# Moving four uses of a shared matmul bank between slots, with other VectorE positions and more filler products, in an attention and expert kernel

## The reference

```python
q, k, v = heads(ln(x) @ Wq + bq), heads(ln(x) @ Wk + bk), heads(ln(x) @ Wv + bv)
y  = softmax(causal(q @ k.T / sqrt(8))) @ v
qc, kc, vc = heads(ln(x) @ Wcq + bcq), heads(ctx @ Wck + bck), heads(ctx @ Wcv + bcv)
y += softmax(qc @ kc.T / sqrt(8)) @ vc
x  = x + y @ Wp + bp
h  = ln(x)
shared = silu(h @ w1.T) * (h @ w2.T) @ w3.T
scores = sigmoid(h @ router.T); top 2 of scores + expert_bias
x  = x + shared + sum over chosen experts of gate * expert(h)
```

## Time and profile before

| | us |
|---|---|
| median of 3 runs | 451.9 (451.32 to 452.56) |
| profiled execution, its time | 452.91 |
| its span, first to last instruction | 451.2 |
| TensorE busy | 401.8 |
| VectorE busy | 351.0 |
| ScalarE busy | 195.8 |
| GpSimd busy | 77.4 |

### The profile page before, as it was taken

One profiled execution on the slowest core, in us unless ns is written; L12 is line 12 of the kernel. 1 busy time (PEld: TensorE's weight loads), 2 busy tenths in 40 slices (PEclk: granted clock), 3 DMA queues, 4 the chain that ended last, 5 costly groups with the idle time before them and its releaser, 6 DMA issues.

```text
span 451.2 us, 10427 instructions
## 1 busy us (share of the span) xinstructions
PE 401.8 (89%) x3759; PEld 298.0 (66%) x3759; DVE 351.0 (78%) x1186; ACT 195.8 (43%) x326; POOL 77.4 (17%) x139
## 2 busy tenths in 40 slices
PE   0579998999899989999899998999889998998986
PEld 0457565667577667767577756767577766765986
DVE  4477676855898877996989787987889788884877
ACT  5135554453433554355443544553444553444221
POOL 4012001400222021210222013110231003201120
PEclk9999899967899998999999989999899999999999
DMA  5631101110201111110201110110101110000000
GB/s 145 198 103 39 54 25 61 58 31 1 84 0 55 48 42 41 41 41 17 81 0 52 47 54 27 52 47 6 64 8 49 42 59 15 1 25 0 2 13 12
DMA packets 28478, 19.63 MB, mean 44 GB/s; under 512 B 6680, under 2 KB 26272, under 8 KB 28448
## 3 DMA queue, kind: packets, MB, share of 16 engines
q1 hardware_dynamic: 27296, 19.02, 13.0%
q10 hardware_dynamic: 1152, 0.20, 0.4%
HBM read 5.58 MB, written 1.05 MB: 15 GB/s over the span
## 4 chain that ended last, share of the span: by engine, by line
PE 51%; DVE 26%; ACT 12%; issue 8%; DMA 1%; SPq 1%; DVEq 0%; POOL 0%; ACTq 0%; POOLq 0%
PE Y L574 10%; ACT probs L793 8%; PE Bk L426 8%; PE Cb L426 6%; DVE masked_s L1030 6%; PE S L450 5%; PE A L426 4%; DVE act L915 4%; DVE shifts L1036 4%; PE Cb L657 3%; PE S L468 3%; ACT th L773 3%; DVE qs L1005 2%; DVE acc L955 2%; PE Y L541 2%
## 5 line engine op out<-in xcount | busy, mean ns | idle before, releaser
L793 ACT ACTIVATE probs<-S 128x1024 f32<-128x1024 f32 (+1 forms) x128 | 112.3, 917 | 54.1 <-PE S L452 53.4
L780 ACT COPY yT<-Y 128x256 f32<-128x256 f32 x64 | 23.9, 373 | 133.8 <-PE Y L574 133.8
L1036 DVE TENSOR_REDUCE shifts<-S 128x4 f32<-128x1024 f32 x64 | 75.2, 1216 | 1.0 <-PE S L468 0.7
L574 PE MATMUL Y<-probs,vs 128*32 128x256 f32 (+1 forms) x1024 | 67.4, 384 | 9.2 <-DVE qs L1005 6.9
L1030 DVE CUSTOM_DVE_ANT_0 masked_s<-S,later_keys 128x256 f32<-128x256 f32 (+1 forms) x256 | 73.4, 352 | 1.4 <-PE S L464 1.3
L915 DVE SCALAR_TENSOR_TENSOR act<-th,A 128x512 f32<-128x512 f32 x42 | 28.7, 683 | 38.2 <-ACT th L773 38.1
L450 PE MATMUL S<-qs,qk 32*128 32x256 f32 x256 | 46.5, 398 | 10.1 <-DVE shifts L1030 7.6
L1080 POOL TENSOR_SCALAR_AFFINE_SELECT probs<-probs 128x1024 f32<-128x1024 f32 x32 | 35.2, 1100 | 108.5 <-ACT probs L793 108.5
L574 PEld LDWEIGHTS Y<-probs,vs 128*32 128x32 f32 x1024 | 27.9, 114 | 34.2 <-DVE qs L1005 17.4
L426 PEld LDWEIGHTS Bk<-w3T,hid 128*128 128x128 f32 x336 | 41.5, 194 | 13.0 <-DVE hid L924 12.2
L426 PE MATMUL Bk<-w3T,hid 128*128 128x128 f32 x336 | 49.2, 290 | 0.6 <-DVE hid L924 0.6
(11 more groups left out here) (148 smaller groups left out, 689.5 us busy)
## 6 DMA issues: line engine op xcount, KB each, us to landing
qk<-nat SPq DMA_DIRECT2D x192, 64.0 KB, 1.9
xin<-in_x_dram SPq DMA_DIRECT2D x8, 128.0 KB, 2.3
w_raw<-in_L_ffn_w_dram SPq DMA_DIRECT2D x4, 256.0 KB
xres<-in_x_dram SPq DMA_DIRECT2D x8, 128.0 KB, 2.3
out_dram<-acc SPq DMA_DIRECT2D x8, 128.0 KB, 1.8
cin<-in_ctx_dram SPq DMA_DIRECT2D x8, 64.0 KB, 2.0
w_raw<-in_L_ffn_shared_w_dram SPq DMA_DIRECT2D x4, 128.0 KB
w_raw<-in_L_ffn_w_dram SPq DMA_DIRECT2D x1, 512.0 KB
```

The costliest lines, as they stand in the source:

```text
L574: mm = nc.tensor.matmul(Y[QUAD * j:QUAD * (j + 1), q0:T], vs[:, kind, kt, GH * g + j, :], probs[u % 2][:, j, kt * T:(kt + 1) * T - q0], st ...
L793: nc.scalar.activation(probs[s % 2][:, hs, 0:kept(s)], S[:, hs, 0:kept(s)], ACT.Exp, scale=SCALE).then_inc(exped[s], 1)
L1036: nc.vector.tensor_reduce(dst.rearrange("p q j -> p j q"), S[:, hs, :].rearrange("p j (q k) -> p j q k", q=NT), AX_X, ALU.max).then_inc(re ...
```

## The change

Of the uses of bank Cb, cT goes from late in slot 4 to early in slot 4, v from early in slot 5 to late in slot 4, and qkc from early in slot 6 to early in slot 7. TensorE makes the early use in slots without a pair too, ahead of the transposed maxima. On VectorE the activation stands behind qs in all slots with a pair; the statistics of the first layer norm go from slot 7 to the start of slot 6, `compare` stands behind them ahead of qs, `choose` goes to the end of slot 7, and the addition of qkc stands between the two halves of slot 7's maxima. GpSimd's `rstd` for the first layer norm and both steps of `route` are in slot 6. The fillers get a count for each half: in slot 7 one in the second half of the scores and one in each half of the maxima; in turn 0, and in turn 1 up to slot 4, slot 4 has two where it had one.

```diff
@@ -54,8 +54,8 @@
-EARLY = [("xT", 1), ("tokens3", -1), ("yT", -1), ("vc", 0), None, ("v", 1), ("qkc", 1), None]
-LATE = [("tokens2", -1), ("qk", 1), ("out", -1), ("x2T", -1), ("cT", 1), ("route", -1), ("tokens0", 0), ("tokens1", 0)]
+EARLY = [("xT", 1), ("tokens3", -1), ("yT", -1), ("vc", 0), ("cT", 1), None, None, ("qkc", 1)]
+LATE = [("tokens2", -1), ("qk", 1), ("out", -1), ("x2T", -1), ("v", 1), ("route", -1), ("tokens0", 0), ("tokens1", 0)]
 C_USES = [use for s in range(SLOTS)
           for use in (EARLY[s], LATE[s]) if use]
@@ -84,7 +84,9 @@
-WARM_EXP, WARM_MAX, FIRST_WARM = {3: 1, 4: 2, 5: 1}, {4: 1}, 1
+WARM_EXP = {3: (1, 1), 4: (2, 2), 5: (1, 1), 7: (0, 1)}
+WARM_MAX = {4: (1, 1), 7: (1, 1)}
+FIRST_WARM = {4: 2}
 class Turn:
@@ -482,14 +484,14 @@
                     nc.tensor.matmul(bank[:, 0:T], ident_bf[:, :], causal[:, :].unsqueeze(1).broadcast_to([P, 2, P]),
                                      start=True, stop=True)
-            def keep_warm(turn, s, counts):
+            def keep_warm(turn, s, half, counts):
                 if turn.at(0) and s >= 2 or turn.at(1) and s <= 4:
-                    bank, n = Bk, FIRST_WARM
+                    bank, n = Bk, FIRST_WARM.get(s, 1)
                 elif turn.loop or turn.t >= 2 or turn.at(1) and s > 5:
-                    bank, n = A, counts.get(s, 0)
+                    bank, n = A, counts.get(s, (0, 0))[half]
                 else:
                     return
                 fill(bank, n)
@@ -501,7 +503,7 @@
                         if half == 0:
                             wait(pe, shifted[s], turn.n(0))
-                        keep_warm(turn, s, WARM_EXP)
+                        keep_warm(turn, s, half, WARM_EXP)
                         un, on = shift_of(s)
                         if turn.has(on):
@@ -549,7 +551,7 @@
                     if turn.at(-1) and u == 0:
                         pe.wait_ge(consts_dve, 2)
                     for half in range(2):
-                        keep_warm(turn, s, WARM_MAX)
+                        keep_warm(turn, s, half, WARM_MAX)
                         if turn.has(0):
                             wait(pe, exped[s], turn.n(0, half + 1, 2))
@@ -688,6 +690,7 @@
                         if turn.has(pair_of(s)[1]):
                             w3_product(turn, pair_of(s))
                     else:
+                        bank_c(turn, EARLY[s])
                         shift_rows(turn, s)
                         maxima(turn, s)
                         values(turn, s)
@@ -993,11 +996,11 @@
                     if not late:
                         from_bank_c(turn, EARLY[s])
                     pr = pair_of(s)
-                    if pr and turn.has(pr[1]):
-                        activate(turn, pr)
-                    if s == 7 and turn.has(2):
+                    if s == 6 and turn.has(2):
                         wait(dve, x_in, turn.n(2, 16, 16))
                         normalise(turn, 2, ln1, 0, 6, xin, stats1, mv1, xn, rstd1_ready, rstd1, True)
+                    if s == 6 and turn.has(-1):
+                        compare(turn, -1)
                     u, o = shift_of(s)
                     if turn.has(o):
@@ -1005,16 +1008,22 @@
                         nc.vector.tensor_tensor(qs[:, u % 2, :], qk[:, u, 0, :].bitcast(F32), Y[:, :],
                                                 ALU.subtract).then_inc(shifted[u], 1)
                     if pr and turn.has(pr[1]):
+                        activate(turn, pr)
+                    if pr and turn.has(pr[1]):
                         times_h2(turn, pr)
-                    if late:
+                    if late and s < 7:
                         from_bank_c(turn, EARLY[s])
                     if s == 3 and turn.has(-1):
                         normalise(turn, -1, ln2, 1, 7, x1, stats2, mv2, x2n, rstd2_ready, rstd2, False)
                     u, o = max_pass(s)
+                    if s == 7 and not turn.has(o):
+                        from_bank_c(turn, EARLY[s])
                     if turn.has(o):
                         for half in range(2):
                             hs = slice(2 * half, 2 * half + 2)
+                            if s == 7 and half == 1:
+                                from_bank_c(turn, EARLY[s])
                             if u < NG:
                                 wait_apart(dve, scores[u], turn.n(o, half + 1, 4), dve_passed)
                             else:
@@ -1038,10 +1047,6 @@
                                                         AX_X, ALU.max).then_inc(reduced[u], 1)
                     if pr and turn.has(pr[1]):
                         add_up(turn, pr)
-                    if s == 6 and turn.has(-1):
-                        compare(turn, -1)
-                    if s == 7 and turn.has(-1):
-                        choose(turn, -1)
                     if turn.at(0):
                         for i in [i for i in raw_banks(s) if i < PAIRS]:
                             dve.wait_ge(raw_hi, i + 1)
@@ -1054,6 +1059,8 @@
                         wait(dve, xT_ps, turn.n(1))
                         normalise(turn, 2, ln1, 0, 6, xin, stats1, mv1, xn, rstd1_ready, rstd1, False)
                     from_bank_c(turn, LATE[s])
+                    if s == 7 and turn.has(-1):
+                        choose(turn, -1)
             def drain(turn):
                 for step, i in DRAIN:
@@ -1148,10 +1155,13 @@
                         for tt in range(NT):
                             r_ = nc.gpsimd.tensor_tensor(xresb[:, tt, :], xres[:, tt, :], bias_row[:, 2, :], ALU.add)
                         r_.then_inc(xresb_ready, 1)
-                    if s in (6, 7) and turn.has(-1):
-                        route(turn, -1, s - 6)
-                    if s == 7 and turn.has(2):
-                        rstd(turn, 2, ln1, 4, 6, mv1, var1, rstd1, rstd1_ready)
+                    if s == 6:
+                        if turn.has(-1):
+                            route(turn, -1, 0)
+                        if turn.has(2):
+                            rstd(turn, 2, ln1, 4, 6, mv1, var1, rstd1, rstd1_ready)
+                        if turn.has(-1):
+                            route(turn, -1, 1)
             turns(pool, one_turn)
```

## The result

The changed kernel takes 495.26 us (median of 4 runs, 493.02 to 495.44) where the kernel before takes 452.23 (4 runs): the ratio is 1.095 (95% interval 1.090 to 1.099). Forecast were 468 in a range of 455 to 482: the sign was right, the size was not. Executions of one kernel differ by several us, as the clock of TensorE falls in more or fewer places; medians and ranges are over all of them, a ratio is over those within 1.5% of the kernel's fastest, and no ratio is given where too few are left. The profiled execution took 495.44 us around a span of 493.7, 42.5 more than the span of before.

What follows compares the result with a forecast made beforehand. VectorE's order was taken to be on the path in slots 0 to 3 and 7, TensorE to set the pace in 5 and 6. Work +22.2, clock -9.0 and +3.0 gave +16.2 us: 468 (463 to 471), eight in ten within 455 to 482.

Steps and rivals of the forecast that it cites:

- The walk's waits: Steady turn: TensorE waits 0.43 for maxima and 0.94 for Cb in slot 4; VectorE over 1 us in slot 7.
- a rise of over 3: Sign to look for: VectorE's idle time rises by over 3 us a turn.
- +3.5: Whole steady turn: the edits add 3.5 us, so 49.44 becomes 52.9.
- The activation in slots 0 to 3: Slots 0 to 3: activation behind qs delays hid and the maxima, +1.94 us a turn.
- Slots 4 to 7: Bank moves and what goes with them: slots 4 to 6 together +0.05 us, slot 7 +1.5 us a turn.
- Fillers and clock: Clock over the whole run: fillers return 9.0 us, new brief falls in slot 4 cost 3.0; 22.2 becomes +16.2.
- term of 3.0: Slot 4: three brief clock falls from TensorE's new waits, at 1.0 us each.
- 9.0 of clock: Fillers holding the clock return turn 1's 5.0, its brief fall 1.0 and three more brief falls 2.9.
- a rival of chance 0.12: Slot 4: the clock falls for long, 5.0 us in each of four turns; 485 us (478 to 490), chance 0.12.
- TensorE is the bound everywhere: All slots: moved products gain, the later activation costs nothing, the clock is held; about 440 us, chance 0.11.
- Half hidden: Activation and slot 7 delays half covered by TensorE's queue and waits: +1.5 a turn, 456 us, chance 0.14.
- the fillers do less than said: Slot 7: low clock stays since fillers shorten no wait; brief falls as often as now, 471 to 477, chance 0.20.

Runs made afterwards that it cites:

- e1: Changed kernel with eight more fillers ahead of TensorE's wait for bank Cb in slot 4: 478.3 us, ratio 1.061.
- e5: Changed kernel with the activation ahead of qs again, all else as changed: 476.3 us (461.2 to 487.8), no ratio.
- e4: Changed kernel with cT late in slot 4 and v early in slot 5 again: 474.0 us, ratio 1.045 against the kernel before.
- e3: Kernel before with the new filler counts alone: 446.6 us, ratio 0.988.
- e6: Kernel before with only cT moved early and v late in slot 4: 476.6 us, ratio 1.056.
- e9: Kernel before with cT early and v late in slot 4, plus eight fillers ahead of the wait for Cb there: 461.5 us, ratio 1.026.
- e2: Kernel before with only the activation moved behind qs, in all slots with a pair: 486.0 us (472.3 to 497.9), no ratio.
- e12: Kernel before with the activation behind qs in slots 5 and 6 alone: 470.5 us (463.9 to 477.1), no ratio.
- e11: Kernel before with new fillers, statistics, comparison and GpSimd's steps in slot 6, late gates, and more fillers in slots 7 and 3: 445.1 us, ratio 0.985.

## Why the prediction was wrong

**Right: what bounds the kernel, and the sign.** VectorE's order is on the path, and moving the activation behind the wait that covered it costs. The walk's waits stand in the trace: in slot 4 TensorE 0.30 for the maxima (0.43 forecast) and 0.95 for the bank (0.94), in slot 7 VectorE 1.63 for the shifts (over 1). VectorE's idle time in a turn is 11.6 us at nearly full clock (54.58 less 42.96 in e1) against 7.3 (49.44 less 42.17), and a rise of over 3 had been named as the sign.

**Right in its mechanism, too small: the work of a turn at full clock.** +3.5 was forecast; with 54.2 it is +4.8. The activation in slots 0 to 3 stood at 1.94 and costs 2.76: from qs of slot 0 to x2T the changed kernel takes 27.80, e5 with the activation ahead 25.04, and the kernel before 25.04 too (223.71 to 248.75). It is 0.65 to 0.72 in each of the four slots, where the forecast took off up to 0.23 for what hides it, and a term was missing, hid's bare wait for the activation's semaphore, 0.11 in a slot. Slots 4 to 7 took 2.0 instead of 1.55; alone, qkc's group cost 0.66 and cT with v 1.5. Over the six turns the work is 28.5 us, where 20.2 stood in the sum. (e1's six turns take 328.4. Six brief falls in slot 7 at 0.37 and one in slot 1 at 1.5, where qs of slot 1 to qs of slot 2 takes 8.1 against 6.6 in e4 at full clock, leave 324.7. The six turns of before at full clock are 296.2, from 50.46 in e3, four times 49.44 and 47.98.)

**Wrong: the step "Fillers and clock", its term of 3.0.** The sum took 9.0 of clock off and put 3.0 on, three brief falls in slot 4 at 1.0. The 9.0 was right: 305.0 less 296.2 is 8.8 for the six turns of before. The 3.0 should have been 24.5: the changed kernel's six turns take 349.2, and 324.7 without low clock. It was mis-sized twice. In number: every turn from 1 to 6 loses the clock in slot 4, not three of them, and three more falls came in slots 7 and 1, 3.6 us together. In length: a fall in slot 4 lasts some 10 us (7 in turn 3) and costs 2.5 to 4.1, and not 1.0. Without the 24.5 the changed kernel would have taken some 471 us, an estimate inside the range, so this term is what put the time outside it.

The mechanism had been named, with turn 1 of before as its price, as a rival of chance 0.12. Its 485 was still short, since it counted four turns and the work was short by 8.3; its 5.0 a turn was more than any of these falls cost. The row that should have decided was at hand: turn 1's long stretch began in slot 4 after less waiting than the walk itself put there (1.37), so the nearest row said long, and the forecast took the farther one. It had waited 0.58 and then 0.41:

```profile
92.74 0.38 PE L450 MATMUL S<-qs,qk 32*128 32x256 f32 x2 [0.41 <-DVE shifts L1036]
```

**The balance.** Error of the span, 42.5 - 16.2 = 26.3: clock in the changed kernel 21.5, work of the six turns 8.3, clock of before 0.2, and -3.7 for what lies around the turns (1.7 less instead of 2.0 more; turn 0 lost its low stretch, and that the late cT hid behind its other work is likely but was not looked at). So the error would have been larger but for what lies around the turns, and that part is luck.

The Trainium skill ("TensorE: Matmul & The Clock Gate", section Terms) prices throttled time at its length times one less the clock ratio, by estimate 5.0 for ten microseconds at half the clock. Here e6 against e9 gives 3.6 a turn, and turn 4 of the changed kernel against its turn at full clock 3.9. A brief fall is 3.4 us long by its row (4.00 x 0.42 x 2; the prediction read 3.8), 1.7 by the rule, and costs 0.96 in slot 7 of the kernel before and 0.37 in slot 7 of e1. So the rule is an upper bound in these rows. That other engines set part of each stretch would explain the difference; no run separates it.

**Rivals.** "TensorE is the bound everywhere" fell with e2. "Half hidden" fell with e1 and e12. That the fillers do less than said is half true: they hold turn 1 and some of slot 7 (e3).

**Open.** Why the clock stays low for 10 us in slots 4 and 5 while TensorE is busy throughout, and for some 3.4 in slot 7, no run here tells. Nor is it settled what brings the long stretch without a wait for the bank: in turns 2 and 6 of e4, in turn 5 of e12, and in turn 1 of the changed kernel.

## What to carry to other kernels

An engine that waits anyway is the place for work that is ready; before moving an operation behind a wait, look whether it filled that wait, and count its whole length (0.60, and 0.11 for the wait of its reader) in each slot, unless its own input comes as late as that wait ends (slots 5 and 6 of the changed kernel). Before putting a use of a shared bank ahead of others, ask when the use before it is released: here 0.95 us of standing TensorE cost 1.5 us of work and 3.6 of clock a turn. When a wait is added to TensorE, price the clock from the longest low stretch that followed a like wait in the same place, and count it in every repetition. What a fall costs in one place is no price for another: the same brief fall cost 0.96 in slot 7 of one kernel and 0.37 in slot 7 of the other.

## What the runs showed of the hardware

- Eight products that nobody reads, in a wait of 0.95 us, decided over some 10 us of half clock: 54.59 against 50.95 a turn (e6, e9).
- The wait is not needed for it: in e4 the clock fell for some 10 us in turn 2 and not at all in turn 5, behind the same waits of TensorE (0.46 and 0.30), and in e12 behind one of 0.24.
- TensorE, 1.00 busy in each microsecond from 325 to 335 by the records, did not get its clock back in that time.
- The activation on VectorE is followed by hid, which waits for its semaphore, 0.71 us after its start (e2), and by qs, which does not, 0.60 after it (0.59 in slot 5 of turn 3 of the kernel before).
- The time of a kernel near such a fall is not one number: e11 ran between 440.1 and 469.1 us, e2 between 472.3 and 497.9.
